# Two heads of each score group accumulate the difference to the other two on their PSUM bank, and two products of zeros precede the turned maxima

## The reference

```
q = (Q @ Wq.T + bq).reshape(Bq, Lq, N_HEADS, D_K).transpose(0, 2, 1, 3)
k = (K @ Wk.T + bk).reshape(Bq, Lk, N_HEADS, D_K).transpose(0, 2, 1, 3)
...
scores = jnp.einsum('bhqd,bhkd->bhqk', q, k) / jnp.sqrt(jnp.float32(D_K))
mask = attn_mask[None, None, :, :]
scores = jnp.where(mask == 0, jnp.float32(-jnp.inf), scores)
attn = jax.nn.softmax(scores, axis=-1)
out = jnp.einsum('bhqk,bhkd->bhqd', attn, v)
...
x = x + _L0_xattn_ref(_layernorm(x, axis=-1), ctx_1024, ctx_1024, ..., mask_SxS2_ik0)
x = x + _L0_ffn_ref(_layernorm(x, axis=-1), L0_ffn_Wg, ...)
```

## Time and profile before

| | us |
|---|---|
| median of 3 runs | 307.57 (305.07 to 308.53) |
| the profiled execution, its own time | 307.24 |
| span of the profiled execution, first to last instruction | 305.4 |
| PE busy | 273.2 (1836 instructions) |
| DVE busy | 205.6 (723) |
| ACT busy | 149.5 (313) |
| POOL busy | 142.4 (229) |
| DVE row maxima, L563 | 55.6 (128 of 476 ns), 36.3 idle before them |
| PE score products, L1150 | 45.5 (128 of 411 ns) |
| PE row masks, L1149 | 38.3 (128 of 305 ns) |
| PE key masks, L1175 | 24.8 (64 of 388 ns) |

### The profile page before, as it was taken

The page is one execution under the profiler, slowest core; times in us unless marked ns, Lnnn a source line. Parts: engine busy times, 40 slices in busy tenths (PEclk is TensorE's granted clock), DMA queues, the critical chain, the costliest instruction groups (busy, mean ns, idle before and its releaser), DMA issues.

```text
span 305.4 us, 6071 instructions
## 1 busy us (share of the span) xinstructions
PE 273.2 (89%) x1836; PEld 206.2 (68%) x1836; DVE 205.6 (67%) x723; ACT 149.5 (49%) x313; POOL 142.4 (47%) x229
## 2 busy tenths in 40 slices
PE   7777899999998999989998999999689999999920
PEld 7654456656556555655564567888589999999920
DVE  2767646665668678765797468782357787886864
ACT  2414687657573655655554744322234644554400
POOL 3546433724433126844338403756006666766660
PEclk9799999999999999999999999999999999999975
DMA  6999940667892000000001100118714968868176
GB/s 211 377 367 397 406 167 3 67 71 95 250 393 95 0 3 0 27 28 17 2 0 36 38 1 2 52 35 240 231 36 129 291 206 260 281 203 262 48 254 206
DMA packets 28495, 44.22 MB, mean 145 GB/s; under 512 B 2752, under 2 KB 16192, under 8 KB 28464
## 3 DMA queue, kind: packets, MB, share of 16 engines
q1 hardware_dynamic: 21808, 36.52, 35.8%
q0 software_dynamic: 6656, 7.31, 10.8%
HBM read 27.00 MB, written 14.73 MB: 137 GB/s over the span
## 4 chain that ended last, share of the span: by engine, by line
PE 62%; DVE 16%; DMA 10%; issue 5%; POOL 5%; ACT 2%; DVEq 0%; POOLq 0%; ACTq 0%; SPq 0%
DVE mpad L563 6%; PE ps L1191 5%; PE ps L1415 5%; PE ps L1421 5%; PE ps L1149 5%; PE ps L1432 5%; PE ps L1177 5%; DMA result_rows<-yo,dest 4%; PE ps L1187 4%; PE ps L1150 4%; PE ps L1175 4%; POOL slot_rows L841 3%; PE ps L1162 3%; PE ps L1099 2%; PE ps L1205 2%
## 5 line engine op out<-in xcount | busy, mean ns | idle before, releaser
L563 DVE TENSOR_REDUCE mpad<-ps 128x2 f32<-128x312 f32 x128 | 55.6, 476 | 36.3 <-PE ps L1150 36.0
L913 POOL DMA_INDIRECT result_rows<-yo,dest x47 | 45.1, 960 | 39.5 <-DVE yo L765 37.4
L791 POOL TENSOR_SCALAR ks<-k_stack,cst 128x160 fp32r<-128x160 f32 x64 | 30.1, 482 | 70.3 <-DVE k_stack L548 70.2
L978 ACT ACTIVATE pf<-ps 128x512 f32<-128x512 f32 x80 | 46.5, 596 | 15.4 <-PE ps L1191 10.9
L1150 PE MATMUL ps<-ks,qs 96*128 96x312 f32 x128 | 45.5, 411 | 0.0
L1149 PE MATMUL ps<-mq_b,identb 128*128 128x312 bf16 x128 | 38.3, 305 | 4.9 <-DVE mpad L563 2.4
L841 POOL DMA_INDIRECT slot_rows<-xr,slot x32 | 31.4, 983 | 14.2 <-issue 13.9
L1177 PE MATMUL ps<-qs,ks 128*128 128x512 f32 x64 | 37.2, 583 | 0.0
L1149 PEld LDWEIGHTS ps<-mq_b,identb 128*128 128x128 bf16 x128 | 12.3, 96 | 32.7 <-issue 26.9
L1086 ACT ACTIVATE e_s<-ps,wu 128x128 f32<-128x128 f32 x62 | 19.4, 363 | 22.0 <-PE ps L1415 22.0
L1432 PE MATMUL ps<-wd,e_h 128*128 (+1 forms) x188 | 29.0, 277 | 1.1 <-DVE yo L765 1.1
(11 more groups left out here) (184 smaller groups left out, 605.1 us busy)
## 6 DMA issues: line engine op xcount, KB each, us to landing
wu<-w_biased SPq DMA_DIRECT2D x31, 322.0 KB, 4.4
wr<-w_up SPq DMA_DIRECT2D x1, 5152.0 KB, 25.1
w_biased<-wr SPq DMA_DIRECT2D x1, 5152.0 KB, 16.8
slot_rows<-zero SPq DMA_DIRECT2D x1, 3120.0 KB, 27.4
xg<-slot_rows SPq DMA_DIRECT2D x12, 260.0 KB, 3.4
wd<-w_down SPq DMA_DIRECT2D x1, 2048.0 KB, 11.9
xo<-result_rows SPq DMA_DIRECT2D x3, 512.0 KB, 5.1
xs<-bor POOLq DMA_DIRECT2D x1, 1024.0 KB, 11.3
```

What stands on the lines that cost most here:

```text
L563: dve.tensor_reduce(mpad[:, m % 2, q, 96 + 2 * a:98 + 2 * a], ps[:, KS_ + a, 0:2 * SKM].rearrange("p (c k) -> p c k", c=2), AX.X, ALU.max, ...
L913: pool.indirect_dma_start(out=result_dram[:, :], out_offset=bass.IndirectOffsetOnAxis(ap=dest[:, n:n + 1], axis=0), in_=yo[:, n % 4, :], i ...
L978: act.activation(pf[:, n % RP, :], ps[:, ST_ + n % 2, :], ACT.Exp, scale=DK ** -0.5).then_inc(exp_done, 1)
```

## The change

Heads 2 and 3 are no longer computed from scratch. Their copies in `ks` hold the head's features minus those of head 0 or 1 (and row 96+j minus row 94+j), and their products are added to a bank on which the masked scores of head 0 or 1 stand already, after these have been read. So half of the mask products are gone, in `score_rows` and in `scores`. A step of `score_rows` now takes one pair of heads for two blocks of query rows: steps 0 and 2 take heads 0 and 1 with masks, steps 1 and 3 heads 2 and 3 without. `row_max` follows that order. `ksl` still holds whole heads, so POOL makes it from `k_stack` in two products rather than from `ks` in one. `turn_max` issues two products of zeros into its bank ahead of its wait for the last maxima, and its other waits now stand ahead of these. The constant table is 100 columns longer.

```diff
-C_END = C_LAST + 32
+C_HEAD = C_LAST + HG * 32
+C_END = C_HEAD + HG
...
+        kl_part = sa("kl_part", [P, HG, 32])
...
             def key_stack(b, m):
                 reach(dve, k_part_done, b, 4, m + 1)
                 reach(dve, ks_done, b, 16, 4 * m - 4)
+                reach(dve, kl_picked, b, 4, m - 1)
...
-            def row_max(b, m, q):
+            def row_max(b, m, step):
-                for a in range(2):
-                    reach(dve, smax_mm, b, 32, 8 * m + 2 * q + a + 1)
-                    dve.tensor_reduce(mpad[:, m % 2, q, 96 + 2 * a:98 + 2 * a],
-                                      ps[:, KS_ + a, 0:2 * SKM].rearrange("p (c k) -> p c k", c=2),
+                a = step % 2
+                for i in range(2):
+                    reach(dve, smax_mm, b, 32, 8 * m + 2 * step + i + 1)
+                    dve.tensor_reduce(mpad[:, m % 2, step // 2 * 2 + i, 96 + 2 * a:98 + 2 * a],
+                                      ps[:, KS_ + i, 0:2 * SKM].rearrange("p (c k) -> p c k", c=2),
                                       AX.X, ALU.max, negate=True).then_inc(max_done, 1)
...
-                reach(pool, ks_done, b, 16, 4 * m + 4)
-                pool.tensor_tensor(ksl[:, m % 4, :, :], ks[:, HG * (m % 4):HG * (m % 4) + HG, P:SKP].bitcast(F32),
-                                   cst[:, C_LAST:C_LAST + 32].unsqueeze(1).to_broadcast([P, HG, 32]),
+                reach(pool, ksl_done, b, 4, m)
+                pool.tensor_tensor(kl_part[:, :, :], k_stack[:, m % 2, P:SKP].unsqueeze(1).to_broadcast([P, HG, 32]),
+                                   cst[:, C_HEAD:C_HEAD + HG].unsqueeze(2).to_broadcast([P, HG, 32]),
+                                   ALU.mult).then_inc(kl_picked, 1)
+                reach(pool, kl_picked, b, 4, m + 1)
+                pool.tensor_tensor(ksl[:, m % 4, :, :], kl_part[:, :, :],
+                                   cst[:, C_LAST:C_LAST + HG * 32].rearrange("p (j i) -> p j i", j=HG),
                                    ALU.add).then_inc(ksl_done, 1)
...
-            def score_rows(b, m, q):
+            def score_rows(b, m, step):
...
-                for a in range(2):
-                    reach(pe, max_done, b, 32, 8 * m + 2 * q + a - 1)
-                    o = ps[:, KS_ + a, 0:2 * SKM].rearrange("p (c k) -> p c k", c=2)
-                    h = HG * (m % 4) + 2 * a
-                    pe.matmul(o, identb[:, :], mq_b[:, q:q + 1, :].to_broadcast([P, 2, SKM]), start=True, stop=False)
+                a = step % 2
+                h = HG * (m % 4) + 2 * a
+                for i in range(2):
+                    q = step // 2 * 2 + i
+                    reach(pe, max_done, b, 32, 8 * m + 2 * step + i - 1)
+                    o = ps[:, KS_ + i, 0:2 * SKM].rearrange("p (c k) -> p c k", c=2)
+                    if a == 0:
+                        pe.matmul(o, identb[:, :], mq_b[:, q:q + 1, :].to_broadcast([P, 2, SKM]), start=True, stop=False,
+                                  skip_group_check=True)
                     pe.matmul(o, qs[0:96, m % 4, P * q:P * q + P], ks[0:96, h:h + 2, 0:SKM],
...
             def turn_max(b, m):
-                reach(pe, max_done, b, 32, 8 * m + 8)
                 reach(pe, qmax_done, b, 4, m)
...
+                for i in range(2):
+                    pe.matmul(ps[:, M_, 0:P], zero[:, 0:P], zero[:, P:2 * P], start=True, stop=True)
+                reach(pe, max_done, b, 32, 8 * m + 8)
...
-                    pe.matmul(o, identb[:, :], mk_b[:, :], start=True, stop=False)
+                    if t <= 2:
+                        pe.matmul(o, identb[:, :], mk_b[:, :], start=True, stop=False, skip_group_check=True)
                     lhs = ks[:, HG * g + t - 1, 0:P]
...
-        c[:, C_SELM + j] = (p < 96) & ((p % 32) // DK == j)
-        c[:, C_SELO + j] = p == 96 + j
+        c[:, C_HEAD + j] = (p < 96) & ((p % 32) // DK == j)
+        before = j - 2 if j >= 2 else -1
+        c[:, C_SELM + j] = c[:, C_HEAD + j] - ((p < 96) & ((p % 32) // DK == before))
+        c[:, C_SELO + j] = (p == 96 + j) * 1.0 - ((before >= 0) & (p == 96 + before))
```

More of the change, by code:

```diff
@@ L237, in build @@
          x2_done, tx_mm, xgt_done, meta_done, gate_mm, lin_mm, esilu_done, eh_done,
-         ey_mm, yo_done, out_done, stored, ld_wk, ld_wq, ld_xr, ld_cr, ld_wr, pool_cleared, bias_done, wlo_done, scaled, routing_set, wk_split, biased, w_kept, y_summed, ld_d, ln_eps, half_set, bo_added) = (sem(n) for n in (
+         ey_mm, yo_done, out_done, stored, ld_wk, ld_wq, ld_xr, ld_cr, ld_wr, pool_cleared, bias_done, wlo_done, scaled, routing_set, wk_split, biased, w_kept, y_summed, ld_d, ln_eps, half_set, kl_picked, bo_added) = (sem(n) for n in (
             "ld_x ld_c ld_w ld_m ld_ctx ld_b zeroed dve_step cleared scanned "
@@ L245, in build @@
             "silu_done h_done w2_mm x2_done tx_mm xgt_done meta_done "
-            "gate_mm lin_mm esilu_done eh_done ey_mm yo_done out_done stored ld_wk ld_wq ld_xr ld_cr ld_wr pool_cleared bias_done wlo_done scaled routing_set wk_split biased w_kept y_summed ld_d ln_eps half_set bo_added").split())
+            "gate_mm lin_mm esilu_done eh_done ey_mm yo_done out_done stored ld_wk ld_wq ld_xr ld_cr ld_wr pool_cleared bias_done wlo_done scaled routing_set wk_split biased w_kept y_summed ld_d ln_eps half_set kl_picked bo_added").split())
         ld_f = [sem(f"ld_f{par}") for par in range(2)]
@@ L1139, in values @@
                 last.then_inc(v_mm, 1)
-            def score_rows(b, m, q):
+            def score_rows(b, m, step):
                 reach(pe, qs_done, b, 4, m + 1)
                 reach(pe, ks_done, b, 16, 4 * m + 4)
-                for a in range(2):
-                    reach(pe, max_done, b, 32, 8 * m + 2 * q + a - 1)
-                    o = ps[:, KS_ + a, 0:2 * SKM].rearrange("p (c k) -> p c k", c=2)
-                    h = HG * (m % 4) + 2 * a
-                    pe.matmul(o, identb[:, :], mq_b[:, q:q + 1, :].to_broadcast([P, 2, SKM]), start=True, stop=False)
+                a = step % 2
[7 more added lines that the diff above has]
+                                  skip_group_check=True)
                     pe.matmul(o, qs[0:96, m % 4, P * q:P * q + P], ks[0:96, h:h + 2, 0:SKM],
-                              start=False, stop=True).then_inc(smax_mm, 1)
+                              start=False, stop=True, skip_group_check=True).then_inc(smax_mm, 1)
             def turn_max(b, m):
-                reach(pe, max_done, b, 32, 8 * m + 8)
                 reach(pe, qmax_done, b, 4, m)
@@ L1174, in scores @@
                 else:
-                    pe.matmul(o, identb[:, :], mk_b[:, :], start=True, stop=False)
+                    if t <= 2:
+                        pe.matmul(o, identb[:, :], mk_b[:, :], start=True, stop=False, skip_group_check=True)
                     lhs = ks[:, HG * g + t - 1, 0:P]
-                pe.matmul(o, lhs, qs[:, g, :], start=t == 0, stop=True).then_inc(st_mm, 1)
+                pe.matmul(o, lhs, qs[:, g, :], start=t == 0, stop=True, skip_group_check=True).then_inc(st_mm, 1)
             def weighted(b, m, t):
@@ L1473, in constants @@
     c[0:NE, C_FIRST] = e
-    for i in range(32):
-        c[96 + HG + min(i, SK - P), C_LAST + i] = 1
+    for j in range(HG):
+        c[96 + j, C_LAST + 32 * j:C_LAST + 32 * j + 32] = 1
+        for i in range(32):
+            c[96 + HG + min(i, SK - P), C_LAST + 32 * j + i] = 1
     c[:, C_TILE:C_TILE + TILES] = np.arange(TILES)
```

## The result

The changed kernel takes 311.25 us (median of 20 executions, 307.54 the fastest) against 309.11 for the kernel before, timed beside it: a ratio of 1.0063, 95% interval 1.0034 to 1.0092 (disturbed executions are left out of this ratio, of those below and of the clock means, so they are not quite quotients of the medians). It is slower by 0.6%. The forecast was 303.8, with 300.5 to 307.3 as the range: the sign is wrong, and the time lies outside. Of the 7.45 us between forecast and result 1.5 belong to the start: the forecast counted from a median of three runs, 307.57, and twenty give 309.11. The other 5.9 are the forecast gain of 3.8 that did not come and the loss of 2.1.

What follows compares the result with a forecast made beforehand. PE and DVE waiting on each other between score steps were taken to bound plain attention units. Gains 0.7 + 0.1 + 3.55 less 0.5 for opening and table made 3.85, say 3.8 us: 303.8 us, range 300.5 to 307.3.

Steps and rivals of the forecast that it cites:

- The clock: Rival, opening and idle stretches of units 0 and 9: less PE work lowers granted clock; from seven stretches about 311; chance 0.06.
- the queue-bound units: Units 0, 7, 9, 11, 13, where DVE's queue holds other work between maxima: gain 0.1 us in all.
- add work in just those gaps: Reason against a clock fall: the two zero products per unit, 0.44 us, were said to fill PE's idle gaps.
- S3 to TM: Fourth score step to turned maxima in a unit: PE's 1.56 us against DVE's 1.39 to 1.43, overrun about 0.15.
- The covered load of TM: First weight load of the turned maxima, hidden after zeros: 0.50 against 0.36 in a stream, cancelling the 0.15 overrun.
- The zeros at 0.22 each: Two zero products per unit, after query products, before the last maxima's wait: 0.44 a unit, 7.1 us over sixteen.
- T0 to T1: First to second head-product step in a unit: ACT no longer holds the second, 0.43 becomes about 0.30, gain 0.13.
- The loop: PE and DVE alternating from second score step to turned maxima in plain units: 1.12, 1.07 and 1.43 us.
- S2 to S3: Third to fourth score step in plain unit 4: bound by PE and DVE together, stays at 1.05 to 1.1 us.
- Split maxima: DVE's row maxima: the same 128 reductions, two per step, only their order changed; cost 0.
- DVE's waits for PE at the maxima: Sign of being right: these waits get longer, since PE no longer fills its alternation with DVE; no size given.
- The opening's T0: Opening, zeros behind the wait for value rows: turned maxima 0.45 us later, cost once (0.44 to 0.56).

Runs made afterwards that it cites:

- filled, no zeros: Changed kernel with zero products filling PE's idle stretches (units 0, 7, 11, opening), without the two ahead of each unit's turned maxima; 304.95 us, 0.9897 of before.
- the filled kernels: Changed kernel with zero products in idle stretches of units 0, 7, 11 and the opening: 305.89 us; likewise without the two ahead of turned maxima: 304.95 us.

## Why the prediction was wrong

**The step that failed: "The clock", chance 0.06.** The sum put the clock at nothing. The mechanism was on the list of rivals, with the opening and "the idle stretches of units 0 and 9" as its place, and with its price: "four such stretches would eat 3.8". There were four, two in unit 0 (the first behind the opening's waits), one in unit 7 and one in unit 11 (unit 9 had none), and they cost 5.4; each lasted 3.4 us where the prediction took 2. The size was near; the chance was not. Two reasons were given against it, and both fail. That the clock held "through idle gaps of 1 us" said nothing on the gaps of the changed kernel, which the removal lengthens to 1.61: the masks cost nothing in the queue-bound units, since idle time hides them, but with all of them (before, twice), or with either kind put back, the clock held in units 7 and 11 in every profile whose DVE queue was left as it was. And the zeros do not "add work in just those gaps": in units 7 and 11 they stand behind S3, past the idle stretch, and in the opening behind the wait for the value rows. The Trainium skill ("TensorE: Matmul & The Clock Gate", Part 1) says that the chip watches PE's activity in a window that runs by itself and does not start with the kernel, so that the point of a change varies between executions. The opening of the unaltered kernel before, once 1.00 and once 0.50, and the two units behind 1.60 and 1.61 us agree with that; no run here was made to test it.

**The gains: mostly the right places, too large by 2 us.** In the units that kept the clock the changed kernel gains (us):

| unit | forecast | changed | filled, no zeros |
|---|---|---|---|
| 1, 2, 3 | 0.45, 0.63, 0.75 | 0.18, 0.35, 0.38 | 0.21, 0.59, 0.51 |
| 5, 6 | 0.62, 0.42 | 0.63, 0.24 | 0.57, 0.38 |
| 10, 14 | 0.42, 0.26 | 0.16, 0.34 | 0.33, 0.28 |
| 4, 8, 12 | 0.23 each | 0.03, -0.07, -0.05 | 0.16, 0.08, 0.08 |
| 9, 13 | next to nothing | 0.10, 0.09 | 0.02, 0.03 |

Together 2.4 in place of 4.35. The mis-sized term is S3 to TM. I took "S3's two products and their load about 0.42", and with Q and zeros 1.56; unit 4 has 0.55 + 0.70 + 0.44 = 1.69 from S3's first product, against 1.40 before, and 0.03 more from its load. What the term left out is a wait inside S3: its second product needs the second bank, which DVE's second maximum on S2 frees at 68.75, and its load, 0.19 like the first, is exposed there once more. Before, that load ran beneath a mask. The covered load of TM does show (0.44 in place of 0.50), but it does not cancel an overrun of 0.29. The zeros at 0.22 each were right (69.76 to 70.20 for two), and so was T0 to T1, 0.32. Without the zeros units 2, 3, 4, 8 and 12 get back 0.8 of the 1.4 that they lack. The forecast had weighed the Trainium skill's figure for an exposed weight load (the same page, Part 2, "LDWEIGHTS (loading the stationary operand)"), by which up to 2.6 us more would have been gained. Nothing of that showed: each of S3's loads still takes 0.19 us, and the measurement decides.

**What held.** The loop bounded the plain units: S2 to S3 stayed at 1.10, and PE's 16.6 us of removed masks did not come off the time. Split maxima and GpSimd's product cost nothing that shows: no PE instruction waited for the last keys' stack, and the filled kernels, which keep both, are the fastest. One sign did not come: DVE's waits for PE at the maxima were to be longer, and went from 36.0 to 34.9 us. The opening's T0 came 0.12 later instead of 0.45, but that stretch had begun 0.3 us earlier (S0 at 15.64 in place of 15.94), so the term was right.

**The sum over again.** 2.4 gained in the units, 0.1 lost in the opening, 5.4 lost to the clock: 3.1 us, as T0 of unit 15 shows (169.49 to 172.57). The end is 4.5 later, but the end is no good measure of two single profiles: from the last product of the experts to the end of the span the first profile of before takes 12.8 us, the second 15.6, and the changed kernel 15.6 in both. The 2.1 us between the medians, or 0.6% by the ratio, is what counts.

## What to carry to other kernels

Work that an engine does in the shadow of a wait can still have a use: on PE it may be what keeps the clock, and taking it away makes the idle stretch longer. Whoever removes PE work should list the idle stretches that get longer and ask what follows them; a few products of zeros put into those stretches themselves, ahead of the wait, turned a loss of 0.6% into a gain of 0.5% here, and 1.0% with the zeros behind the wait taken out. A filler that stands behind the wait did not keep the clock here, and is paid for wherever PE is the later one. And a term of zero in the sum, the clock's here, needs a reason that holds for the changed kernel, not only for the one before.

## What was not expected of the hardware

An idle stretch of PE of 3.00 us was followed by full clock, and others of 1.25 us (unit 0, halved row masks) by 3.4 us of half clock. With full row masks around the idle stretch the fall was rarer. With S3's masks alone back it fell in one unit of two, so the work right behind the idle time does not decide by itself, and in the stage after attention it fell behind 1.93 us and not behind 2.12 of the same wait. What decides stays open: longer idle time and less work around it go with the fall, and unaltered kernels differ from one execution to the next. The runs separate these kernels by how often the clock falls, not by a rule.
